# Attention with a mixture of experts: the inverse sums are spread over the partitions by two transfers through DRAM in place of transposes and a copy, with another order of the attention's steps

## The chip, the cores and the metric

The kernel runs on one core of one Trainium2 chip. The metric is the time of one execution on the device, in microseconds. The core has five engines with a queue each: TensorE (PE; its weight loads are PEld), VectorE (DVE), ScalarE (ACT), GpSimd (POOL) and SyncE (SP). They meet in semaphores. 16 DMA engines carry all transfers.

## The reference

One transformer layer on 2048 tokens of 512 values: attention with 16 heads of 128, a layer norm, then a mixture of 64 experts (6 chosen for each token) with shared experts, and a second layer norm. The change touches the attention alone:

```python
k = einsum('ihd,bpd->biph', W_K, x)       # q and v alike
scores = einsum('biph,biqh->biqp', k, q)
masked = scores * tril - 1e10 * (1 - tril)
attn = softmax(masked / sqrt(128), axis=-1)
z = einsum('biqp,biph->biqh', attn, v)
out = einsum('df,bqf->bqd', W_O, z_flat)
```

## The kernel before

The attention runs over eight pairs of heads, `i`, with an unrolled body for each. In a pair, h is the head (0 or 1) and c one of four chunks of 512 queries; (h, c) is a unit, and the units go (0,0), (1,0), (0,1), (1,1), ... (1,3). Every float32 operand is split in a high part and a low part, and each product is three matmuls (high x high, high x low, low x high).

The steps of a pair are:

- "job": projections of q, k and v of a chunk. They write one of four PSUM banks (`bank`), which ScalarE (L375) and VectorE (L466) split.
- "s": a score tile of 128 queries (r) by 512 keys (kc), in a bank too (L606). VectorE takes its maximum (L481), and at the end of a row the maximum of the parts (L487) and its negated, scaled value (L489). "exp" is ScalarE's exponential with the running sum (L391).
- "turn": 128 x 128 transposes of the probabilities of key tile j, up to four, into `turned` (L623). ScalarE copies the high part `pT_hi` (L402), and "lo" is VectorE's low part `pT_lo` (L495). "pv" is the value product of tile j, three matmuls into `z_ps` (L638). A unit of chunk c has 4(c + 1) tiles; the last three of them are cut to 384, 256 and 128 columns by the causal mask.
- "inverse": VectorE adds a unit's sums (L506) and takes the reciprocal (L508), 128 x 4 numbers. They lie with the query on the partition, while `z_ps` has the query along the columns.
- "norm": so TensorE transposes each of the four columns, broadcast to 128 x 128, into a bank (L651), and ScalarE copies the bank to `spread_sb` (L410).
- "out": VectorE multiplies `z_ps` by `spread_sb` into `z_sb` (L516), and SyncE stores it (L336). `z_ps` is one bank: the next unit's first value product waits for this step.

Each engine runs its own share of the steps in the order of one string, `ORDER`: "f" stands for the next projection or score, "e" exp, "t" turn, "l" lo, "p" pv, "i" inverse, "n" norm, "o" out and "w" the split of the next pair's weights. There are no priorities besides it, so what stands behind a waiting instruction on its engine waits too. Chunk 0 of the next pair is projected and scored ahead, in the body before.

SyncE also loads each chunk of x (two transfers of 1 MB, L277 and L278) after the last v projection of the chunk before, and in three of the four places zeroes two or three blocks of `gathered_x`, rows of 527 values, behind them (L322). GpSimd only makes constants in this stage. After the attention comes a stage with the output projection, the routing and the experts, and then the combination of the sums.

Of the kernel before, what the change touches and what calls it, by code (L numbers as in the profile page):

```python
# [7 lines left out]
P = 128  # L8
# [55 lines left out]
def wait_apart(eng, waited, sem, value):  # L64
# [12 lines left out]
    "tttflillffffifnffpteeflfpteffeeeppttolnffleeptffleepfftlepeffpettfeolllffepeitplfiffntlfffffptpetept"  # L77
    "llefflptfppeolfeettffepltfepelftlfpltleeptlenpfpfttlffeepptoetlffpelteefpllftfppelieettptnlflfflptee"
    "ffefflfffffpftppettellptlefppotltlffpleftlptipetpeeelltfpffftleepeletpfffftpleeeeltppfffflttlpeepnel"
    "ottfplletffflpwtpetllpetfleptefplffwwteeepptltfflflpetplfppwieetleettllffppttpltpilnfltlofffpetlppft"  # L80
    "tefellpefffftepelpfttleptllfptptplltptplltptllpnpepo"
# [3 lines left out]
def attention_plan():  # L85
# [7 lines left out]
    for h in range(2):  # L93
# [6 lines left out]
        "n": [("norm", 0, *unit) for unit in units], "o": [("out", 0, *unit) for unit in units],  # L100
# [8 lines left out]
def attention(nc, xT, x_parts, w_qkv, z_dram, gathered_x, sums_dram):  # L109
# [7 lines left out]

    ahead_steps = [step for step in plan if step[1]]
# [6 lines left out]
    jobs = [step for step in plan if step[0] in ("job", "s", "norm")]  # L125
    job_at = counted("job", "s", "norm")
    proj_at, exp_at, lo_at = counted("job"), counted("exp"), counted("lo")
    turn_at, pv_at, unit_at = counted("turn"), counted("pv"), counted("out")
    assert counted("inverse") == unit_at and counted("norm") == unit_at
# [16 lines left out]
    with ExitStack() as ctx:  # L146
# [6 lines left out]
        def sem(name):  # L153
            return ctx.enter_context(nc.semaphore(name))
# [9 lines left out]
        spread_sb = sb("spread_sb", [P, CHUNK], F32)  # L164
# [4 lines left out]
        empty_row = sb("empty_row", [P, ROW], F32)  # L169
# [36 lines left out]
        spread_done = sem("spread_done")  # L206
# [50 lines left out]
        @block.gpsimd  # L257
        def _(pool):
            nc.gpsimd.memset(empty_row[:], 0.0).then_inc(const_step, 1)
            nc.gpsimd.memset(ident[:], 0.0).then_inc(const_step, 1)  # L260
            nc.gpsimd.memset(causal_bf[:], 0.0).then_inc(const_step, 1)
            pool.wait_ge(const_step, 3)

            nc.gpsimd.iota(empty_row[:, TOKEN:TOKEN + 1].bitcast(I32), pattern=[[0, 1]], base=SEQ,
                           channel_multiplier=1).then_inc(pool_const, 1)
# [3 lines left out]
            nc.gpsimd.affine_select(out=causal_bf[:], in_=causal_bf[:], compare_op=ALU.is_ge, fill=MASKED,  # L269
                                    base=0, pattern=[[-1, P]], channel_multiplier=1).then_inc(pool_const, 1)  # L270

        @block.sync
        def _(sp):
# [66 lines left out]
            sp.dma_start(sums_dram[SEQ:SEQ + P], empty_row[:, 0:DM]).then_inc(zero_out, 16)  # L340
            sp.wait_ge(x_in, 32 * (CHUNKS * PAIRS - 1))
            sp.wait_ge(zero_out, 16 * (EXPERTS + 1))
# [4 lines left out]
        def _(act):  # L347
# [23 lines left out]
            act.sem_inc(spread_done, n_units)  # L371
# [33 lines left out]
            def spread(i, h, c):  # L405
                u = unit_at[h, c]
                act.wait_ge(job_ready, upto(i, n_jobs, job_at["norm", h, c]))

                act.wait_ge(z_done, upto(i, n_units, u - 1))
                nc.scalar.activation(spread_sb[:], bank[:, job_at["norm", h, c] % BANKS], ACT.Copy).then_inc(spread_done, 1)  # L410

            def body(i, last):
                for step in steps_of(last):
# [6 lines left out]
                    if step[0] == "norm":  # L420
                        spread(i, *step[2:])
# [15 lines left out]
        def _(dve):  # L437
# [61 lines left out]
            def inverse(i, h, c):  # L499

                u = unit_at[h, c]
                before = (c - 1) % CHUNKS
# [41 lines left out]
        def _(pe):  # L544
# [7 lines left out]
            def take(i, n, last):  # L552
# [9 lines left out]
                elif kind == "norm":  # L562
                    pe.wait_ge(spread_done, upto(i, n_units, unit_at[tuple(old)], m < 0))
# [98 lines left out]
            def body(i, last):  # L662
                for step in steps_of(last):
# [8 lines left out]
                    if step[0] == "norm":  # L672
                        spread(i, *step[2:], last)
# [1294 lines left out]
def post_ln_layer(nc, xT, x_rows, w_qkv, w_o, gate_w, w13, w2, s13, s2, out):  # L1968
# [3 lines left out]
    x_parts = dram("x_parts", [CHUNKS, 2, P, DT * CHUNK])  # L1972
    z_dram = dram("z_dram", [TILES, P, HEADS, P])
# [4 lines left out]
    attention(nc, xT, x_parts, w_qkv, z_dram, gathered_x, sums_dram)  # L1978
# [48 lines left out]
```

## Time and profile before

| | |
|---|---|
| time, median of three runs | 2611.55 us (2609.22 to 2616.04) |
| time of the profiled execution | 2612.08 us |
| its span in the trace | 2610.3 us |
| TensorE busy | 2474.8 us, 95% |
| VectorE busy | 1762.7 us, 68% |
| ScalarE busy | 1454.5 us, 56% |
| GpSimd busy | 268.6 us, 10% |
| mean of the granted TensorE clock | 0.983 |

The busy times are those of the whole span. A time in the trace counts from the start of the span; 1.8 us of the execution lie around it. The attention ends at about 1665 us.

### The profile page before, as it was taken

Reading aid. Unit: us, or ns where it says so; the run is one execution under the profiler, and the core shown is the slowest. Engines: PE = TensorE matmul, PEld = TensorE weight load, DVE = VectorE, ACT = ScalarE, POOL = GpSimd, SP = SyncE. Lnnn points to the kernel's source line nnn. Section 1 sums busy time; section 2 is a strip of 40 time slices with the busy share of each in tenths; the row PEclk is TensorE's granted clock in tenths of the full one; section 3 lists DMA queues with packets and bytes.
Section 4 is the critical chain, followed back from the end, with each engine's and each line's share of the span. In section 5 each row is a group of like instructions: output and inputs, shape, how many; then the busy total and the mean of one; then the engine's idle time right before and its main releaser. Section 6 shows DMA issues by size and latency. Waiting matters only on the chain. (4 is left out here: it accounts for less than half of the span.)

```text
span 2610.3 us, 40937 instructions
## 1 busy us (share of the span) xinstructions
PE 2474.8 (95%) x14304; PEld 2141.0 (82%) x14304; DVE 1762.7 (68%) x3802; ACT 1454.5 (56%) x3247; POOL 268.6 (10%) x221
## 2 busy tenths in 40 slices
PE   6999999999999999999999999798899999999992
PEld 5888888888888888888888888576688889898992
DVE  4666566566566557557567566588867888888884
ACT  3555555455456456456456455444436777777771
POOL 0000000000000000000000000045551112122121
PEclk9999999999999999999999999899999999999996
DMA  6311311310320320311311220367749999999995
GB/s 250 124 49 47 120 49 47 123 51 15 118 88 15 108 86 27 108 54 55 108 58 55 82 66 18 144 219 269 248 134 278 308 295 317 305 299 318 303 310 154
DMA packets 176892, 380.09 MB, mean 146 GB/s; under 512 B 19561, under 2 KB 52457, under 8 KB 166448
## 3 DMA queue, kind: packets, MB, share of 16 engines
q1 hardware_dynamic: 154096, 330.69, 37.4%
q0 software_dynamic: 20288, 42.59, 7.1%
q10 hardware_dynamic: 2304, 4.20, 0.4%
q8 instruction: 115, 1.88, 0.3%
q14 instruction: 89, 0.73, 0.1%
HBM read 279.67 MB, written 106.35 MB: 148 GB/s over the span
## 5 line engine op out<-in xcount | busy, mean ns | idle before, releaser
L402 ACT ACTIVATE pT_hi<-turned 128x512 fp32r<-128x512 f32 (+3 forms) x640 | 330.4, 537 | 292.1 <-PE turned L623 291.1
L495 DVE TENSOR_TENSOR pT_lo<-turned,pT_hi 128x512 fp32r<-128x512 f32 (+3 forms) x640 | 375.5, 604 | 104.9 <-ACT pT_hi L402 102.9
L391 ACT ACTIVATE probs<-bank,neg_max 128x512 f32<-128x512 f32 (+3 forms) x640 | 395.9, 626 | 80.2 <-DVE neg_max L489 76.1
L481 DVE TENSOR_REDUCE max_part<-bank 128x1 f32<-128x512 f32 (+2 forms) x576 | 344.8, 621 | 114.5 <-PE bank L606 103.7
L593 PE MATMUL bank<-x_sb,w_hi 128*128 128x512 f32 x1024 | 323.4, 397 | 20.1 <-ACT ident_bf L366 13.6
L623 PE MATMUL turned<-ident,probs 128*128 128x128 f32 x2176 | 320.5, 273 | 0.3 <-PEq L682 0.3
L623 PEld LDWEIGHTS turned<-ident,probs 128*128 128x128 f32 x2176 | 263.1, 141 | 44.9 <-issue 0.7
L638 PE MATMUL z_ps<-pT_hi,v_hi 128*128 128x512 f32 (+3 forms) x640 | 255.6, 399 | 14.9 <-DVE pT_lo L495 12.4
L606 PE MATMUL bank<-k_lo,q_hi 128*128 128x512 f32 (+2 forms) x640 | 254.2, 397 | 0.0
L606 PE MATMUL bank<-k_hi,q_hi 128*128 128x512 f32 (+2 forms) x640 | 250.3, 391 | 0.0
L1736 DVE TENSOR_TENSOR up_lo<-w_raw,up_hi 128x704 fp32r<-128x704 f32 x256 | 217.3, 887 | 34.3 <-ACT up_hi L1243 33.3
L593 PEld LDWEIGHTS bank<-x_sb,w_hi 128*128 128x128 f32 x1024 | 191.7, 190 | 59.1 <-issue 13.6
L638 PE MATMUL z_ps<-pT_hi,v_lo 128*128 128x512 f32 (+3 forms) x640 | 234.8, 367 | 0.0
L638 PE MATMUL z_ps<-pT_lo,v_hi 128*128 128x512 f32 (+3 forms) x640 | 234.0, 366 | 0.0
L606 PE MATMUL bank<-k_hi,q_lo 128*128 128x512 f32 (+2 forms) x640 | 233.7, 365 | 0.0
L593 PE MATMUL bank<-x_sb,w_lo 128*128 128x512 f32 x512 | 201.4, 393 | 0.0
L582 PE MATMUL bank<-w_hi,x_sb 128*128 128x256 f32 x1024 | 191.8, 284 | 1.7 <-ACT probs L391 1.7
L1243 ACT ACTIVATE up_hi<-w_raw 128x704 fp32r<-128x704 f32 x250 | 185.0, 786 | 3.1 <-DMA w_raw<-in_w 2.7
L977 POOL MEMSET ident<- 128x128 f32 x1 | 0.2, 204 | 1666.3 <-POOLq L146 1666.3
L582 PEld LDWEIGHTS bank<-w_hi,x_sb 128*128 128x128 f32 x1024 | 162.1, 191 | 3.3 <-DVE probs L454 2.1
L638 PEld LDWEIGHTS z_ps<-pT_hi,v_hi 128*128 128x128 f32 x640 | 121.2, 189 | 36.6 <-DVE pT_lo L495 14.1
L1049 POOL DMA_INDIRECT sums_dram<-y_sb,token x64 | 110.0, 1720 | 386.5 <-DMA sums_dram<-y_sb,token 244.1
(211 smaller groups left out, 5259.4 us busy)
## 6 DMA issues: line engine op xcount, KB each, us to landing
w_raw<-in_w SPq DMA_DIRECT2D x256, 352.0 KB, 5.6
x_sb<-x_parts SPq DMA_DIRECT2D x62, 1024.0 KB, 6.0
w_raw<-in_w SPq DMA_DIRECT2D x128, 256.0 KB, 5.7
gathered_x<-empty_row SPq DMA_DIRECT2D x64, 263.5 KB, 9.3
rows_in<-gathered_x SPq DMA_DIRECT2D x64, 263.5 KB, 5.4
z_dram<-z_sb SPq DMA_DIRECT2D x64, 256.0 KB, 2.3
z_raw<-z_dram SPq DMA_DIRECT2D x16, 1024.0 KB, 5.8
w_raw<-in_w_qkv SPq DMA_DIRECT2D x32, 384.0 KB, 10.5
```

Source lines behind the costliest of these rows:

```text
L391: nc.scalar.activation(probs[:, u % 2, r, kc * CHUNK:kc * CHUNK + used], bank[:, job_at["s", h, c, r, kc] % BANKS, 0:used], ACT.Exp, bias= ...
L402: nc.scalar.activation(pT_sb[0][:, n % TURNS, lo_col:], turned[:, n % TURNS, lo_col:], ACT.Copy).then_inc(turn_hi, 1)
L481: nc.vector.reduce_max(max_part[:, row % ROWS, kc:kc + 1], bank[:, job % BANKS, 0:used], axis=AX_X).then_inc(part_done, 1)
L495: nc.vector.tensor_tensor(pT_sb[1][:, n % TURNS, lo_col:], turned[:, n % TURNS, lo_col:], pT_sb[0][:, n % TURNS, lo_col:].bitcast(F32), AL ...
L582: mark = nc.tensor.matmul(dst[:, t * 2 * DH:(t + 1) * 2 * DH], x_sb[:, a, dt, rows_], w_sb[b][:, dt, 4 * DH:], start=(dt == 0 and (a, b) = ...
L593: mark = nc.tensor.matmul(dst, w_sb[a][:, dt, first:first + DH], x_sb[:, b, dt, :], start=(dt == 0 and (a, b) == PASSES[0]), stop=(dt == D ...
L606: mark = nc.tensor.matmul(dst[:, 0:width], q_sb[a][:, h, r * P:(r + 1) * P], k_sb[b][:, h, kc * CHUNK:kc * CHUNK + width], start=(a, b) == ...
L623: mark = nc.tensor.transpose(turned[:, n % TURNS, r * P:(r + 1) * P], probs[:, u % 2, r, j * P:(j + 1) * P], ident[:])
L638: mark = nc.tensor.matmul(z_ps[:, first * P:], v_sb[a][:, j, h * DH:(h + 1) * DH], pT_sb[b][:, n % TURNS, first * P:], start=(j == 0 and ( ...
L1049: nc.gpsimd.indirect_dma_start(sums_dram, bass.IndirectOffsetOnAxis(ap=token4[:, n:n + 1], axis=0), y_sb[:, n % 2], None, bounds_check=las ...
L1243: nc.scalar.activation(dst_of(0, n % 2, p, up_w, down_w), raw_of(raw, q % SLOTS_RAW, p), ACT.Copy).then_inc(w_hi, 1)
L1736: nc.vector.tensor_tensor(dst_of(1, n % 2, p, up_w, down_w), raw_of(raw, q % SLOTS_RAW, p), dst_of(0, n % 2, p, up_w, down_w).bitcast(F32) ...
```

## The change

The step "norm" goes. In its place GpSimd stores the 128 x 4 inverse sums of a unit in a DRAM row of 512 values, waits until they are there, and loads the row into all 128 partitions of `spread_sb`, which now has two buffers. In DRAM the four values of a partition stand side by side, so the z product reads the row with a step of four values for each of its four blocks of 128 columns. The inverse waits for the store of the unit two before in place of the norm's transposes. The zeros that SyncE writes come from a tile of 271 columns in place of 527, so each such transfer becomes two. The order string is another one.

```diff
 ORDER = (
-    "tttflillffffifnffpteeflfpteffeeeppttolnffleeptffleepfftlepeffpettfeolllffepeitplfiffntlfffffptpetept"
+    "tlfiiftfffltlfffpftlfpppoeeefefttetelffpllteffeeplpfeftetepolfltfilfpfeepttelleffffffpffftptilelptfp"
...
-    jobs = [step for step in plan if step[0] in ("job", "s", "norm")]
+    jobs = [step for step in plan if step[0] in ("job", "s")]
...
+            def spread(i, h, c):
+
+                u = unit_at[h, c]
+                per = 16 * n_units // 2
+                wait_apart(pool, waited, inv_done, upto(i, n_units, u))
+                pool.dma_start(inv_dram[u % 2].rearrange("(p r) -> p r", r=RPC), inv[:, u % 2]).then_inc(inv_stored[u % 2], 16)
+                wait_apart(pool, inv_free, inv_stored[u % 2], i * per + 16 * (u // 2 + 1))
+                wait_apart(pool, waited, z_done, upto(i, n_units, u - 2))
+                pool.dma_start(spread_sb[:, u % 2], inv_dram[u % 2:u % 2 + 1].to_broadcast([P, CHUNK])
+                               ).then_inc(spread_in[u % 2], 16)
...
-                            sp.dma_start(gathered_x[bass.ds(e, 1)].rearrange("a p n -> (a p) n"),
-                                         empty_row[:]).then_inc(zero_out, 16)
+                            empty = gathered_x[bass.ds(e, 1)].rearrange("a p n -> (a p) n")
+                            sp.dma_start(empty[:, 0:EMPTY], empty_row[:, 0:EMPTY]).then_inc(zero_out, 16)
+                            sp.dma_start(empty[:, EMPTY:], empty_row[:]).then_inc(zero_out, 16)
...
-            sp.dma_start(sums_dram[SEQ:SEQ + P], empty_row[:, 0:DM]).then_inc(zero_out, 16)
+            for first in range(0, DM, EMPTY):
+                sp.dma_start(sums_dram[SEQ:SEQ + P, first:first + EMPTY], empty_row[:, 0:EMPTY]).then_inc(zero_out, 16)
...
-            def spread(i, h, c):
-                u = unit_at[h, c]
-                act.wait_ge(job_ready, upto(i, n_jobs, job_at["norm", h, c]))
-
-                act.wait_ge(z_done, upto(i, n_units, u - 1))
-                nc.scalar.activation(spread_sb[:], bank[:, job_at["norm", h, c] % BANKS], ACT.Copy).then_inc(spread_done, 1)
...
-                dve.wait_ge(job_ready, upto(i, n_jobs, job_at["norm", h, before], c == 0))
+                dve.wait_ge(inv_free, upto(i, n_units, u - 2))
                 nc.vector.reduce_sum(total[:, u % 2], sums[:, u % 2, :, 0:c + 1], axis=AX_X).then_inc(sum_done, 1)
...
-                dve.wait_ge(spread_done, upto(i, n_units, u))
-
+                dve.wait_ge(spread_in[u % 2], i * (8 * n_units) + 16 * (u // 2 + 1))
                 dve.wait_ge(z_out[u % 2], i * (8 * n_units) + (8 * n_units + 16 * (u // 2)))
-                nc.vector.tensor_tensor(z_sb[:, u % 2], z_ps[:], spread_sb[:], ALU.mult).then_inc(z_done, 1)
+                by_row = spread_sb[:, u % 2].rearrange("p (n r) -> p r n", r=RPC)
+                nc.vector.tensor_tensor(z_sb[:, u % 2].rearrange("p (r n) -> p r n", r=RPC),
+                                        z_ps[:].rearrange("p (r n) -> p r n", r=RPC), by_row, ALU.mult).then_inc(z_done, 1)
...
-            def spread(i, h, c, last):
-
-                u = unit_at[h, c]
-                dst = take(i, job_at["norm", h, c], last)
-                pe.wait_ge(inv_done, upto(i, n_units, u))
-                for r in range(RPC):
-                    mark = nc.tensor.transpose(dst[:, r * P:(r + 1) * P], inv[:, u % 2, r:r + 1].to_broadcast([P, P]),
-                                               ident[:])
-                mark.then_inc(job_ready, 1 + left_out(i, job_at["norm", h, c], last))
```

How the order moves is seen at the end of unit (1, 2), in each pair. TensorE's program has there before, from the last score tile of the first row of unit (1, 3) to the first matmul of the row's successor (the matmuls on `z_ps` of 256 and 128 columns are the value products of the last two tiles of (1, 2)):

```order
L606 MATMUL bank<-k_lo,q_hi 128x256
L606 MATMUL bank<-k_hi,q_lo 128x256
L623 MATMUL turned<-ident,probs 128x128 x5
L638 MATMUL z_ps<-pT_hi,v_hi 128x256
L638 MATMUL z_ps<-pT_lo,v_hi 128x256
L638 MATMUL z_ps<-pT_hi,v_lo 128x256
L638 MATMUL z_ps<-pT_hi,v_hi 128x128
L638 MATMUL z_ps<-pT_lo,v_hi 128x128
L638 MATMUL z_ps<-pT_hi,v_lo 128x128
L651 MATMUL bank<-ident,inv 128x128 x4
L623 MATMUL turned<-ident,probs 128x128 x8
L606 MATMUL bank<-k_hi,q_hi 128x512
```

And after the change, from the same score tile:

```order
L621 MATMUL bank<-k_lo,q_hi 128x256
L621 MATMUL bank<-k_hi,q_lo 128x256
L638 MATMUL turned<-ident,probs 128x128 x4
L653 MATMUL z_ps<-pT_hi,v_hi 128x256
L653 MATMUL z_ps<-pT_lo,v_hi 128x256
L653 MATMUL z_ps<-pT_hi,v_lo 128x256
L638 MATMUL turned<-ident,probs 128x128 x4
L653 MATMUL z_ps<-pT_hi,v_hi 128x128
L653 MATMUL z_ps<-pT_lo,v_hi 128x128
L653 MATMUL z_ps<-pT_hi,v_lo 128x128
L638 MATMUL turned<-ident,probs 128x128 x4
L621 MATMUL bank<-k_hi,q_hi 128x512
```

The four transposes of inv are gone; the transposes of unit (0, 3)'s first tiles are split up among the last two value products.

On VectorE the same place before, from the maxima of that score row to the z product of unit (1, 2); the three `pT_lo` of 256, 128 and 512 columns are tiles 10 and 11 of (1, 2) and tile 0 of (0, 3):

```order
L481 TENSOR_REDUCE max_part<-bank 128x1 [waits job_ready,exp_done]
L481 TENSOR_REDUCE max_part<-bank 128x1 [waits job_ready] x3
L487 TENSOR_REDUCE row_max<-max_part 128x1 [waits part_done]
L489 TENSOR_SCALAR neg_max<-row_max 128x1 [waits max_done]
L495 TENSOR_TENSOR pT_lo<-turned,pT_hi 128x256 [waits turn_hi]
L495 TENSOR_TENSOR pT_lo<-turned,pT_hi 128x128 [waits turn_hi]
L495 TENSOR_TENSOR pT_lo<-turned,pT_hi 128x512 [waits turn_hi]
L516 TENSOR_TENSOR z_sb<-z_ps,spread_sb 128x512 [waits z_out1,spread_done,pv_done]
```

And after:

```order
L498 TENSOR_REDUCE max_part<-bank 128x1 [waits job_ready,exp_done]
L498 TENSOR_REDUCE max_part<-bank 128x1 [waits job_ready]
L512 TENSOR_TENSOR pT_lo<-turned,pT_hi 128x256 [waits turn_hi]
L498 TENSOR_REDUCE max_part<-bank 128x1 [waits job_ready] x2
L504 TENSOR_REDUCE row_max<-max_part 128x1 [waits part_done]
L506 TENSOR_SCALAR neg_max<-row_max 128x1 [waits max_done]
L512 TENSOR_TENSOR pT_lo<-turned,pT_hi 128x128 [waits turn_hi]
L512 TENSOR_TENSOR pT_lo<-turned,pT_hi 128x512 [waits turn_hi]
L532 TENSOR_TENSOR z_sb<-z_ps,spread_sb 128x512 [waits z_out1,spread_in1,pv_done]
```

Tile 10's low part has moved ahead of the last two maxima; the z product waits for `spread_in1`, a transfer, in place of `spread_done`.

## Rows read from the trace of the kernel before

**Rows 1.** Windows: a middle pair, the last pair, and the gap behind it.

```profile
core 0: us, PE busy (x) PEld busy (x) DVE busy (x) ACT busy (x) POOL busy (x), PEclk, DMA share, GB/s
252.80:456.30 203.50, 202.15 (x1203) 172.44 (x1202) 125.25 (x268) 109.92 (x277) 0.00 (x0) 1.00 0.21 71
1473.80:1664.50 190.70, 185.06 (x1075) 156.84 (x1074) 113.51 (x243) 100.18 (x253) 0.00 (x0) 0.98 0.14 45
1664.50:1680.00 15.50, 0.91 (x2) 0.83 (x3) 5.45 (x8) 5.14 (x5) 1.94 (x8) 0.59 0.77 289
```

**Rows 2.** Timeline, PE, the first spread of two pairs (start, us, what).

```profile
270.38 0.28 PE L582 MATMUL bank<-w_hi,x_sb 128*128 128x256 f32 x1
270.49 0.60 PE L651 MATMUL bank<-ident,inv 128*128 128x128 f32 x4
270.85 0.47 PE L606 MATMUL bank<-k_hi,q_hi 128*128 128x512 f32 x1
271.16 0.39 PE L606 MATMUL bank<-k_lo,q_hi 128*128 128x512 f32 x1
271.38 0.39 PE L606 MATMUL bank<-k_hi,q_lo 128*128 128x512 f32 x1
...
473.97 0.60 PE L651 MATMUL bank<-ident,inv 128*128 128x128 f32 x4
```

**Rows 3.** Groups by line, the middle pair from 252.8 us to 456.3 us.

```profile
line engine op names shapes xcount | busy us, mean ns | idle before us <-releasers
...
L638 PEld LDWEIGHTS z_ps<-pT_hi,v_hi 128*128 128x128 f32 x80 | 15.1, 189 | 3.9 <-DVE pT_lo L495 1.6 <-issue 0.8 <-DVE z_sb L516 0.3
...
L516 DVE TENSOR_TENSOR z_sb<-z_ps,spread_sb 128x512 f32<-128x512 f32 x8 | 5.5, 686 | 2.4 <-issue 1.3 <-PE z_ps L638 1.0
...
L410 ACT ACTIVATE spread_sb<-bank 128x512 f32<-128x512 f32 x9 | 5.4, 605 | 1.6 <-PE bank L651 1.4
```

**Rows 4.** Timeline, end of unit (1, 2) in that pair; in brackets the idle time.

```profile
390.27 0.71 PE L623 MATMUL turned<-ident,probs 128*128 128x128 f32 x5
...
391.11 0.15 DVE L489 TENSOR_SCALAR neg_max<-row_max 128x1 f32<-128x1 f32 x1
391.18 1.21 DVE L495 TENSOR_TENSOR pT_lo<-turned,pT_hi 128x256 fp32r<-128x256 f32 x3
...
391.65 0.39 PE L638 MATMUL z_ps<-pT_hi,v_hi 128*128 128x256 f32 x1 [0.67 <-DVE pT_lo L495]
...
392.39 0.62 PE L651 MATMUL bank<-ident,inv 128*128 128x128 f32 x4
...
392.85 1.04 PE L623 MATMUL turned<-ident,probs 128*128 128x128 f32 x8
...
393.05 0.60 ACT L410 ACTIVATE spread_sb<-bank 128x512 f32<-128x512 f32 x1
...
393.73 0.69 DVE L516 TENSOR_TENSOR z_sb<-z_ps,spread_sb 128x512 f32<-128x512 f32 x1 [1.34 <-issue]
...
394.48 0.19 PEld L638 LDWEIGHTS z_ps<-pT_hi,v_hi 128*128 128x128 f32 x1 [0.33 <-DVE z_sb L516]
```

**Rows 5.** Line 996: GpSimd's plain loads (192 to 352 KB), later stage.

```profile
L996 POOL DMA_DIRECT2D s_raw<-in_s x14: 559/593/782, 1669.9 to 1878.8; - x14
...
DMA to landing us min/median/max: 3.1/4.1/6.6
```

**Rows 6.** Lines 336 (store of z) and 322 (zeros), issue and landing.

```profile
L336 SPq DMA_DIRECT2D z_dram<-z_sb x64: 359/371/378, 74.7 to 1665.2; - x64
...
DMA to landing us min/median/max: 2.3/2.3/8.9
...
DMA to landing us min/median/max: 2.3/9.3/10.7
```

**Rows 7.** Timeline, end of the attention.

```profile
1663.14 0.29 DVE L495 TENSOR_TENSOR pT_lo<-turned,pT_hi 128x128 fp32r<-128x128 f32 x1 [0.28 <-ACT pT_hi L402]
...
1664.12 0.27 PE L638 MATMUL z_ps<-pT_hi,v_lo 128*128 128x128 f32 x1
1664.48 0.69 DVE L516 TENSOR_TENSOR z_sb<-z_ps,spread_sb 128x512 f32<-128x512 f32 x1 [1.04 <-PE z_ps L638]
...
1665.60 0.51 SPq L340 DMA_DIRECT2D sums_dram<-empty_row  x1
```

More of the change, by code:

```diff
@@ L76 @@
 ORDER = (
-    "tttflillffffifnffpteeflfpteffeeeppttolnffleeptffleepfftlepeffpettfeolllffepeitplfiffntlfffffptpetept"
[L78 to L81, printed above, removed]
+    "tlfiiftfffltlfffpftlfpppoeeefefttetelffpllteffeeplpfeftetepolfltfilfpfeepttelleffffffpffftptilelptfp"
+    "lfeetfelppoefettffelepetfplffltpeetlfpffeltpeftplleftfeeppottlfllefpetpfleeepfttpffeitleellfffffffff"
+    "fptptlpetpeetlepltffplfftlelpeetpetofflpfltflptpeetlpieflpfetfltfpteepltptllffppeetlfftpleltpoeltfep"
+    "tlfeplffwtpetpllwtlefptpeltfelpftfiwpeetelptflfeptlflfwepeppteetlltlffpptptlotfplltfffppetlfetfelile"
+    "pffffetlfppttlleepftptllptptplltlptpltelpppo"
 )
@@ L99, in attention_plan @@
         "p": [("pv", 0, *tile) for tile in tiles], "i": [("inverse", 0, *unit) for unit in units],
-        "n": [("norm", 0, *unit) for unit in units], "o": [("out", 0, *unit) for unit in units],
+        "o": [("out", 0, *unit) for unit in units],
         "w": [("wsplit", 0, dt) for dt in range(DT)],
@@ L106, in attention_plan, with attention @@
     return plan, units
-def attention(nc, xT, x_parts, w_qkv, z_dram, gathered_x, sums_dram):
+def attention(nc, xT, x_parts, w_qkv, inv_dram, z_dram, gathered_x, sums_dram):
     plan, units = attention_plan()
@@ L116, in attention @@
     ROWS = 4
+    EMPTY = DM // 2
     ahead_steps = [step for step in plan if step[1]]
@@ L122, in counted @@
                 for n, step in enumerate(step for step in plan if step[0] in kinds)}
-    jobs = [step for step in plan if step[0] in ("job", "s", "norm")]
-    job_at = counted("job", "s", "norm")
+    jobs = [step for step in plan if step[0] in ("job", "s")]
+    job_at = counted("job", "s")
     proj_at, exp_at, lo_at = counted("job"), counted("exp"), counted("lo")
     turn_at, pv_at, unit_at = counted("turn"), counted("pv"), counted("out")
-    assert counted("inverse") == unit_at and counted("norm") == unit_at
+    assert counted("inverse") == unit_at
     rows = [step[2:5] for step in plan if step[0] == "s" and step[5] == 0]
@@ L163, in attention @@
         pT_sb = [sb(f"pT_{n}", [P, TURNS, CHUNK], F32R) for n in ("hi", "lo")]
-        spread_sb = sb("spread_sb", [P, CHUNK], F32)
+        spread_sb = sb("spread_sb", [P, 2, CHUNK], F32)
         z_sb = sb("z_sb", [P, 2, CHUNK], F32)
@@ L168, in attention @@
         causal_bf = sb("causal_bf", [P, P], BF16)
-        empty_row = sb("empty_row", [P, ROW], F32)
+        empty_row = sb("empty_row", [P, ROW - EMPTY], F32)
         max_part = sb("max_part", [P, ROWS, CHUNKS], F32)
@@ L205, in attention @@
         inv_done = sem("inv_done")
-        spread_done = sem("spread_done")
+        inv_stored = [sem(f"inv_stored{n}") for n in range(2)]
+        inv_free = sem("inv_free")
+        spread_in = [sem(f"spread_in{n}") for n in range(2)]
+        waited = sem("waited1")
         z_done = sem("z_done")
@@ L270, in _, with body @@
                                     base=0, pattern=[[-1, P]], channel_multiplier=1).then_inc(pool_const, 1)
+            pool.sem_inc(inv_free, n_units)
+            def spread(i, h, c):
[7 more added lines that the diff above has]
+                               ).then_inc(spread_in[u % 2], 16)
+            def body(i):
+                for step in plan:
+                    if step[0] == "inverse":
+                        spread(i, *step[2:])
+            for i in range(PAIRS):
+                body(i)
         @block.sync
@@ L370, in _ @@
             act.sem_inc(turn_hi, n_turns)
-            act.sem_inc(spread_done, n_units)
             def project(i, job):
@@ L419, in body @@
                         turn(i, *step[2:])
-                    if step[0] == "norm":
-                        spread(i, *step[2:])
                     if step[0] == "wsplit" and not last:
@@ L561, in take @@
                     pe.wait_ge(exp_done, upto(i, n_exp, exp_at[tuple(old)], m < 0))
-                elif kind == "norm":
-                    pe.wait_ge(spread_done, upto(i, n_units, unit_at[tuple(old)], m < 0))
                 else:
@@ L671, in body @@
                         value(i, *step[2:])
-                    if step[0] == "norm":
-                        spread(i, *step[2:], last)
             for step in ahead_steps:
@@ L1972, in post_ln_layer @@
     x_parts = dram("x_parts", [CHUNKS, 2, P, DT * CHUNK])
+    inv_dram = dram("inv_dram", [2, CHUNK])
     z_dram = dram("z_dram", [TILES, P, HEADS, P])
@@ L1977, in post_ln_layer @@
     x1T_parts = dram("x1T_parts", [TILES, 2, P, DT * P])
-    attention(nc, xT, x_parts, w_qkv, z_dram, gathered_x, sums_dram)
+    attention(nc, xT, x_parts, w_qkv, inv_dram, z_dram, gathered_x, sums_dram)
     route_and_experts(nc, z_dram, w_o, gate_w, x_rows, w13, w2, s13, s2, sums_dram, x1T_parts, gathered_x)
```

5 lines of the change are left out of this document (2 added, 3 removed).

## Prediction

> **What bounds the kernel now.** I read the windows first. One of the middle pairs of heads takes 203.5 us, and TensorE is busy for 202.15 us of them, VectorE for 125.25 and ScalarE for 109.92, at a granted clock of 1.00, which is the 2.4 GHz level [rows 1]. The period of a pair is seen a second time in the starts of the same block of transposes, 270.49 and 473.97: 203.48 us [rows 2]. So between 60 and 1640 us the end is set by what TensorE has in its queue. Work that leaves its queue is won in full; work that leaves VectorE or ScalarE is won only where TensorE waits for them.
>
> Then the timeline, because busy time of matmuls is modelled and hides short waits. The distance from one start to the next tells more. In a pair these distances leave about 2.4 us that are no work, and all of it stands at one place, the end of unit (h 1, chunk 2). The piece of it shown in [rows 4] reads so: five transposes are issued at 390.27, and the next in the queue, the value matmul of tile 10 (256 columns), starts at 391.65, with 0.67 us shown as idle. The five need 0.11 us each (four take 0.45 in the row at 392.39), so 0.83 us are lost. The reason stands between: VectorE finishes the maximum of a score row first (the negated maximum, 391.11) and only then makes tile 10's low part (391.18), because its program has the row's four maxima ahead of it. A second, smaller wait comes behind it: the z product starts at 393.73, when the copy of the spread has ended (393.05 plus 0.60), and TensorE's next value matmul starts at 394.48, which is 0.3 us late. The grouped row of one pair says the same: 1.6 us of waiting for pT_lo, 0.8 put down to issue, 0.3 for z_sb [rows 3].
>
> **What goes, and what it costs today.** The spread is four transposes in each of 64 units. [Rows 2]: they start at 270.49, the next matmul at 270.85, so 0.36 us; and that matmul is followed by the next at 271.16, 0.31 us later, where the one after it has 0.22 or 0.23: another 0.08. Together 0.44 us. In the other setting, between transposes, it is 392.39 to 392.85, 0.46 us [rows 4]. I take 0.44: 64 x 0.44 = **28.2 us** off TensorE's queue, all of it on the path, since the queue is 99% full. Eight bank slots in a pair go too, which can only relax the ring of four banks.
>
> ScalarE loses 64 copies of 0.605 us [rows 3], 39 us, or 4.8 us of a pair's 110. It is 46% idle there, so this is worth nothing by itself; it shortens the answers for which TensorE waits at the place above.
>
> **What comes.** Two transfers per unit, issued by GpSimd, which has no other work in this stage (busy 0.00 in [rows 1]). Nothing that TensorE does waits for them directly: the z product on VectorE does, and behind it VectorE's whole queue, and the next unit's first value matmul. So the question is whether they land in the time between the inverse and the z product. In the new list the shortest such stretch is unit (1, chunk 2): six score tiles of 0.69 us (three passes of 0.23), one of 0.82 and one of 0.48, five value tiles of 0.69 and three cut ones of 0.53, 0.36 and 0.32, and transposes for 2.86 us at 0.11 each: 13.0 us of TensorE's work. The next is unit (0, chunk 3), 16.5 us; the others have 18.8 to 29.7. In the last pair, where the steps ahead are missing, units of chunk 3 have 11.1 and 11.9 us plus the waits of that tail.
>
> The trace has no transfer of either kind, so I bound the chain. Below: the fastest store of z, 2.3 us [rows 6], and the fastest GpSimd load, 3.1 us [rows 5]: 5.4. Above: 8.9 and 6.6 us, with two issues of 0.78: 17.1. The slow end of the store belongs to one that is queued behind the loads of x and three zero transfers, which themselves take 9.3 us in the median and at most 10.7 to land [rows 6]; in the new list the inverse of (1, chunk 2) stands 19 us behind the last such burst. So I take a quiet store of 3, a median load of 4.1 and two issues of 0.59: about **8.3 us**, hidden in 13.0 and in 11.1. Cost 0. If the cover were gone, each microsecond over 13.0 would cost 8 us.
>
> VectorE's z product changes shape: it reads the spread with a step of four floats. Today it takes 0.686 us [rows 3]. No row has such a read. Below, it costs nothing (a read with a step has no less to do, so no gain); above, it costs as much again as the product's own streaming: the pT_lo product of 128 columns takes 0.28 to 0.29 and z's of 512 takes 0.69 [rows 7], so 384 columns are 0.40 and 512 are 0.53 us. It matters only where the product is waited for. At the end of the attention the last matmul starts at 1664.12 and the product at 1664.48 [rows 7], 0.36 later; with its 0.69 and 0.06 for the hand-over the next unit's first value matmul can start 1.1 us after the last one's start. The new list puts 0.11 + 1.13 = 1.24 us of work there after unit (1, chunk 2), and 1.8 or more after the others: just enough at 0.69, 0.4 us short at 1.22. I take 0 to 0.4 per pair, 0.2 in the middle: 1.6 us.
>
> Against this stands a rule of the Trainium skill ("SBUF — State Buffer", section "Door 1: The DMA port swizzle", the note on cachelines): SBUF has lines of 16 bytes, full speed needs at least two hits in a line, and each access to a new line pays. A step of four floats meets a new line with every element. By it the product would be at the upper end and the sum 1.6 us higher (an estimate); no row here shows it.
>
> **What moves.** The list is another one, so the 2.4 us of waiting in a pair are drawn anew. On VectorE two of the four maxima of row (1, chunk 3, r 0) now stand behind the low part of tile 10 instead of ahead of it, which takes away the 0.9 us of [rows 4]. The low part of tile 11 still stands behind the row's negated maximum, while TensorE has its value matmul 1.2 us behind that score: I count 0.3 to 0.4 us there. On TensorE the transposes of a tile and the value matmul that needs them stand under 2 us apart in 6 places of a pair instead of 10. That speaks for about 1 us a pair rather than 2.4. But a new list can have places of its own that I don't see from positions, so I count only half of the difference and of that what the z product leaves: 2.4 - 1.6 = 0.8 us a pair, eight times, **6 us**. The product's 0.2 is in these 1.6.
>
> SyncE issues 64 more zero transfers (about 0.5 us each) behind the loads of x. The stores of z behind them come up to 1.6 us later, with two buffers of z and at least 9 us to the next store that needs one: 0. At the very end one more such transfer is issued after the last store: the one that is there starts at 1665.60, takes 0.51 us [rows 7], and the stage's end waits for it: +0.4 us.
>
> **Sum.** The profiled execution took 2612.1 us (0.5 over the median of the three runs shown, 2611.55). 2612.1 - 28.2 - 6 + 0.4 = 2578.3; against the median, 2577.8. I say **2578**.
>
> **Rivals.**
> *The waits all go.* With 0.2 us left in a pair the list is worth 17.6 instead of 6: 2566.5. For it: all waits of today stand at one place, and the list loosens it. Against: tile 11 there. 20 in 100.
> *The saved work is won, but the z product is slow or the list waits as before.* 2612.1 - 28.2 + 0.4 + 8 x 0.4 = 2587.5. For it: the step of four floats and the 1.24 us. 18 in 100.
> *The list has new waits of 3 us a pair on top of today's,* for example where the turn of unit (0, chunk 3) stands 1.3 us behind the exp of its last row instead of 4.1. Then -28.2 + 24: 2608, within 0.3% of no change. 5 in 100.
> *The transfers come too late,* the rival on the other side. VectorE stands at the z product of (1, chunk 2) and (0, chunk 3) while TensorE runs dry behind it. With a chain of L the cost of a pair is (L - 13.0) + (L - 16.5) over zero. It eats the 28.2 us at L = 16.5 and makes the kernel slower by over 0.3% from L = 17.0; at 18 it costs 52 us, and the time is 2636. For it: 128 descriptors that all read the same 2 KB of DRAM, which no row has, and 128 pieces of 16 bytes in the store. Against: L must be twice my value, and the upper bound from rows is 17.1. 7 in 100.
> That the change doesn't do what it says has nothing for it: no transposes of inv are left on TensorE.
>
> **How the numbers follow.** The forecast has 50 in 100. A difference under 0.3%, 8 us, could not be told from none. The range of the forecast alone is 2572 to 2584; to leave out no more than 2 in 10 it takes in the two rivals beside it: 2565 to 2592. Faster 0.88, same 0.05, slower 0.07.
>
> **What the profile of the changed kernel would show.** A pair's window of about 199.5 us with TensorE busy for all but 1 to 2 of them. z product at 0.69 us or up to 1.2. GpSimd's spread landing in 3 to 5 us, its store in 2 to 4, and no idle time of VectorE ahead of the z product that ends with a landing; if there is such a row with more than 0.5 us each, the rival on the other side is at work. The prediction is wrong if the pair's period falls by less than 3.5 us: then a wait took the place of the transposes, and the idle column of the value matmuls names it.

## The result and the profile after

The changed kernel takes 2575.84 us (median of 4; 2568.45 to 2578.61) against 2613.8 us (4 runs) of the kernel before: a ratio of 0.986, 95% interval 0.9841 to 0.9879. Forecast were 2578 and a range of 2565 to 2592. The profiled execution took 2573.6 us with a span of 2571.8.

The windows of a middle pair and of the last pair, with the columns of [rows 1]:

```profile
core 0: us, PE busy (x) PEld busy (x) DVE busy (x) ACT busy (x) POOL busy (x), PEclk, DMA share, GB/s
248.18:446.64 198.46, 198.40 (x1170) 169.40 (x1170) 127.52 (x268) 106.08 (x269) 8.63 (x16) 1.00 0.27 83
1439.00:1621.50 182.50, 179.73 (x1043) 152.07 (x1041) 116.48 (x243) 95.50 (x242) 8.63 (x16) 0.99 0.20 59
```

A pair is 5.0 us shorter (203.5 in [rows 1]) and TensorE shows hardly any idle time in it. VectorE has 2.3 us more work, ScalarE 3.8 less, GpSimd 16 issues. The same pair by line, which answers to [rows 3]:

```profile
line engine op names shapes xcount | busy us, mean ns | idle before us <-releasers
...
L653 PEld LDWEIGHTS z_ps<-pT_hi,v_hi 128*128 128x128 f32 x80 | 15.1, 189 | 2.3 <-DVE z_sb L532 0.5 <-DVE pT_lo L512 0.4
...
L532 DVE TENSOR_TENSOR z_sb<-z_ps,spread_sb 128x512 f32<-128x512 f32 x8 | 8.6, 1081 | 0.9 <-PE z_ps L653 0.8
```

The z product takes 1.08 us in place of 0.69, and its engine never waits for a transfer ahead of it. Of the 3.9 us of idle time ahead of the weight loads of the value matmuls in [rows 3], 2.3 are left; of the part put down to VectorE, 0.9 in place of 1.9. The end of unit (1, 2), as in [rows 4] (timeline):

```profile
383.12 0.36 PE L653 MATMUL z_ps<-pT_hi,v_hi 128*128 128x256 f32 x1
...
383.67 1.05 DVE L512 TENSOR_TENSOR pT_lo<-turned,pT_hi 128x128 fp32r<-128x128 f32 x2
...
384.01 0.33 PE L653 MATMUL z_ps<-pT_hi,v_hi 128*128 128x128 f32 x1
...
384.64 1.08 DVE L532 TENSOR_TENSOR z_sb<-z_ps,spread_sb 128x512 f32<-128x512 f32 x1
...
385.32 0.40 PE L621 MATMUL bank<-k_hi,q_lo 128*128 128x512 f32 x1
...
385.77 0.50 PE L653 MATMUL z_ps<-pT_hi,v_hi 128*128 128x512 f32 x1
```

Tile 10's value matmul (383.12) comes without the 0.83 us wait. The one wait left at this place is at 385.77: 0.45 us after the matmul before it, where 0.23 would do, because the z product ends at 385.72.

The transfers of that unit (timeline):

```profile
371.18 0.18 DVE L524 RECIPROCAL inv<-total 128x4 f32<-128x4 f32 x1
371.93 0.54 POOL L283 DMA_DIRECT2D inv_dram<-inv  x1 [31.71 <-DVE inv L524]
374.29 0.54 POOL L286 DMA_DIRECT2D spread_sb<-inv_dram  x1 [1.82 <-DMA inv_dram<-inv]
```

Over all 64 units, from issue to landing, the store first, then the load:

```profile
DMA to landing us min/median/max: 1.7/1.7/8.4
...
DMA to landing us min/median/max: 3.3/3.5/4.4
```

The reciprocal ends at 371.36 and the spread lands at 374.29 + 3.5 = 377.8: a chain of 6.4 us, while the z product starts 13.3 us behind the reciprocal (its cover). That is a quiet unit. Unit (1, 1) of the same pair stores its sums right behind two loads of x and six transfers of zeros, issued from 301.9 to 305.4 us; the DMA share is 0.92 from 306 to 314 us (timeline):

```profile
305.35 0.18 DVE L524 RECIPROCAL inv<-total 128x4 f32<-128x4 f32 x1
306.11 0.54 POOL L283 DMA_DIRECT2D inv_dram<-inv  x1 [18.58 <-DVE inv L524]
314.26 0.54 POOL L286 DMA_DIRECT2D spread_sb<-inv_dram  x1 [7.62 <-DMA inv_dram<-inv]
325.68 1.09 DVE L532 TENSOR_TENSOR z_sb<-z_ps,spread_sb 128x512 f32<-128x512 f32 x1
```

Its store takes 7.5 us to land, the chain is 12.2 us long and the cover 20.2. The longest chain of the pairs looked at is that of (1, 0) in the last pair, 14.9 us under a cover of 26.0: it stands behind the chain of (0, 0) in GpSimd's queue.

The attention ends (end of the last z product) at 1622.0 us in place of 1665.2, 43 us earlier, but the execution is 38.5 us shorter. Some 3 of the 43 us are the granted clock of the one execution that was traced before. Its last pair holds two stretches at 0.50; the kernel with the split zeros alone (an experiment below), whose attention is otherwise the one of before, has none in its last pair and ends it at 1662.6 us:

```profile
1640.10:1643.50 3.40, 3.40 (x18) 3.30 (x16) 1.24 (x4) 1.10 (x3) 0.00 (x0) 0.50 0.00 0
1646.90:1650.30 3.40, 3.40 (x11) 2.70 (x11) 0.66 (x1) 0.60 (x1) 0.00 (x0) 0.50 0.27 77
...
1471.20:1661.90 190.70, 185.11 (x1096) 156.97 (x1094) 115.30 (x246) 101.68 (x256) 0.00 (x0) 1.00 0.16 51
```

From 1662.6 it is 40.6 us. What lies behind the attention took 945.2 us in the trace of before and 949.9 in this one; the last experiment comes back to this.

### The profile page after: what moved, and what is told of

The parts are those of the page before. It is cut to its first block and busy times, and to the rows that moved or that the text cites. A ratio compares the mean times of both kernels' runs of the same rounds, so it can differ in the third digit from the quotient of the medians.

```text
span 2571.8 us, 40617 instructions
## 1 busy us (share of the span) xinstructions
PE 2444.0 (95%) x14048; PEld 2115.2 (82%) x14048; DVE 1778.3 (69%) x3802; ACT 1423.4 (55%) x3183; POOL 339.3 (13%) x349
## 5 line engine op out<-in xcount | busy, mean ns | idle before, releaser
L608 PE MATMUL bank<-x_sb,w_hi 128*128 128x512 f32 x1024 | 323.9, 398 | 20.0 <-ACT ident_bf L393 13.3
L638 PE MATMUL turned<-ident,probs 128*128 128x128 f32 x2176 | 329.2, 273 | 0.1
L283 POOL DMA_DIRECT2D inv_dram<-inv x64 | 34.9, 546 | 1350.7 <-DVE inv L524 1350.7
L597 PE MATMUL bank<-w_lo,x_sb 128*128 128x256 f32 x512 | 145.5, 284 | 0.0
```

The costliest lines, as they stand in the source:

```text
L597: mark = nc.tensor.matmul(dst[:, t * 2 * DH:(t + 1) * 2 * DH], x_sb[:, a, dt, rows_], w_sb[b][:, dt, 4 * DH:], start=(dt == 0 and (a, b) = ...
L608: mark = nc.tensor.matmul(dst, w_sb[a][:, dt, first:first + DH], x_sb[:, b, dt, :], start=(dt == 0 and (a, b) == PASSES[0]), stop=(dt == D ...
L638: mark = nc.tensor.transpose(turned[:, n % TURNS, r * P:(r + 1) * P], probs[:, u % 2, r, j * P:(j + 1) * P], ident[:])
```

## The experiments

The times of a kernel spread by 10 us, the period of a pair in one trace hardly at all as long as no transfer is late: it was 203.48 us before and 198.46 now, again and again. So the period is compared, measured from a projection of v to the same one of the next pair, and the times stand beside it.

**The transfers alone.** The changed kernel with the order string of before, its eight "n" taken out:

```diff
-    "tlfiiftfffltlfffpftlfpppoeeefefttetelffpllteffeeplpfeftetepolfltfilfpfeepttelleffffffpffftptilelptfp"
+    "tttflillffffifffpteeflfpteffeeeppttolffleeptffleepfftlepeffpettfeolllffepeitplfifftlfffffptpeteptlle"
```

> The changed kernel with the order of before (its eight n taken out), so the transfers without the new list. If TensorE's queue is what counts and the list is a term of its own: the period of a middle pair is 203.5 - 3.5 = 200.0 us, perhaps 0.3 more for the slower z product, and the time about 2612 - 28 = 2584, some 9 to 12 us over the changed kernel. If the whole gain came from the list and the transposes had been hidden: 2612 and a period of 203.5. If the transfers only do no harm thanks to the new list (late ones in the old): over 2600, with idle time of VectorE at the z product that ends with a landing.

Measured: 2589.9 us, ratio 0.9913 (0.9894 to 0.9932). The window of a pair:

```profile
260.76:461.12 200.36, 198.96 (x1169) 169.15 (x1168) 127.32 (x268) 105.85 (x268) 8.65 (x16) 1.00 0.28 83
```

3.12 us less than before. The 0.83 us wait of [rows 4] is there again, and so are the other waits for pT_lo (1.6 us in the pair ahead of the weight loads, as in [rows 3]). The end of unit (1, 2) (timeline):

```profile
384.60 0.71 PE L638 MATMUL turned<-ident,probs 128*128 128x128 f32 x5
385.97 0.39 PE L653 MATMUL z_ps<-pT_hi,v_hi 128*128 128x256 f32 x1 [0.67 <-DVE pT_lo L512]
...
386.60 0.28 PE L653 MATMUL z_ps<-pT_hi,v_lo 128*128 128x128 f32 x1
...
386.91 1.11 DVE L532 TENSOR_TENSOR z_sb<-z_ps,spread_sb 128x512 f32<-128x512 f32 x1 [0.20 <-PE z_ps L653]
...
388.07 0.40 PE L621 MATMUL bank<-k_hi,q_lo 128*128 128x512 f32 x1
388.30 0.40 PE L653 MATMUL z_ps<-pT_hi,v_hi 128*128 128x512 f32 x1
```

But the wait for the z product is gone here: it starts 0.31 us after the unit's last value matmul, where it stood behind ScalarE's copy before (393.73 in [rows 4]), and the next value matmul follows in 0.23 us although the product is slower. That gives 0.2 us back. A new wait of 0.3 us stands at 274.92, at the first value matmul of unit (1, 0): TensorE comes there earlier, without the transposes, and VectorE's low part ends 0.4 us later, behind the slower product of (0, 0). The list is a term of its own, of 200.36 - 198.46 = 1.90 us a pair.

**The transposes doubled,** in the kernel before:

```diff
-                for r in range(RPC):
+                for r in (*range(RPC), *range(RPC)):
```

> The kernel before with the four transposes of the spread issued twice. If each block of four costs its whole 0.44 us of TensorE's queue: period 203.5 + 3.5 = 207.0 us and time 2612 + 28 = 2640. If part of the block lies in waits that are there anyway (TensorE waits 2.4 us in a pair): less, down to 2612 + 20. If the transposes were hidden: 2612.

Measured: 2638.2 us, ratio 1.0087 (1.0068 to 1.0105).

```profile
269.27:476.24 206.97, 205.63 (x1234) 175.91 (x1232) 125.20 (x268) 109.95 (x276) 0.00 (x0) 1.00 0.21 70
```

3.49 us more, 0.436 per block of four: the sum's 0.44. Adding (3.49) and taking away (3.12, and 0.1 for the waits that changed) agree within 0.3 us.

**The list alone.** The kernel before with the new order. It needs eight "n" in it, and they take a place in the ring of four banks. I placed them twice:

```diff
-    "tttflillffffifnffpteeflfpteffeeeppttolnffleeptffleepfftlepeffpettfeolllffepeitplfiffntlfffffptpetept"
+    "tlfiiftnfffltlfffpftlfpppoeneefefttetelffpllteffeeplpfeftetepolfltfilfpfeeptntelleffffffpffftptilelp"
```

> The kernel before (transposes and copy) with the new order, n put in where the bank ring allows it. The list as a term of its own: the period falls by the waiting that it removes, 203.5 - 1.5 = 202.0 us, and the time to about 2600. If the list pays only together with the transfers (because ScalarE has less to do, and no bank is taken): 2609 to 2616, period 203 or more, and the 0.9 us waits of tile 10 come back or move.

Measured: 2668.3 us, ratio 1.0207 (1.0188 to 1.0226), period 211.3. Neither expectation held: TensorE waited for exponentials that free a bank, right at the "n". One such place (timeline):

```profile
425.05 0.40 PE L606 MATMUL bank<-k_hi,q_lo 128*128 128x512 f32 x1
427.80 1.11 PE L651 MATMUL bank<-ident,inv 128*128 128x128 f32 x4 [2.35 <-ACT probs L391]
428.55 0.78 PE L638 MATMUL z_ps<-pT_hi,v_hi 128*128 128x512 f32 x1
429.13 0.63 PE L638 MATMUL z_ps<-pT_lo,v_hi 128*128 128x512 f32 x1
```

> Again the kernel before (transposes and copy) with the new order, but each n later, where the ring of four banks is least strained. In the run before TensorE waited for exponentials that free a bank at six places, 8 us a pair, right where the n stood. If that was the place of the n alone: period 202 to 202.5 us, 2600 to 2605. If the new list needs the ring without the eight spread jobs: the waits for exponentials come back elsewhere and the period stays over 204.

Measured with the later places: 2609.0 us, ratio 1.0008 (0.9994 to 1.0022), period 203.8, no better than before. The expectation's second branch, with a period over 204, fits in kind, but not quite in size. The waits for pT_lo are gone (0.2 us in place of 1.6), but others stand around the spread of (1, 2):

```profile
393.63 0.65 PE L651 MATMUL bank<-ident,inv 128*128 128x128 f32 x4 [0.56 <-ACT probs L391]
...
395.64 0.50 PE L606 MATMUL bank<-k_hi,q_hi 128*128 128x512 f32 x1 [0.61 <-ACT probs L391]
```

So with these places of "n" the new list is worth nothing while the spread takes a bank, and 1.9 us a pair once it takes none. Whether some other placement would have kept a part of it is open; 2 of many were tried. Nor is it shown whether the bank or ScalarE's eight copies (0.6 us each) make the exponentials late here: both runs have both.

**The step of four.** The store writes column by column, so that the z product reads its row packed:

```diff
-                pool.dma_start(inv_dram[u % 2].rearrange("(p r) -> p r", r=RPC), inv[:, u % 2]).then_inc(inv_stored[u % 2], 16)
+                pool.dma_start(inv_dram[u % 2].rearrange("(r p) -> p r", r=RPC), inv[:, u % 2], allow_slow_non_contiguous=True).then_inc(inv_stored[u % 2], 16)
...
+                nc.vector.tensor_tensor(z_sb[:, u % 2], z_ps[:], spread_sb[:, u % 2], ALU.mult).then_inc(z_done, 1)
```

> The changed kernel, but the store writes the 128 x 4 numbers column by column (512 pieces of 4 bytes), so that the z product reads its row packed. If the step of four floats makes the product slow: 0.69 us in place of 1.08, the 0.2 us wait of TensorE for the z product goes, period 198.46 - 0.2 to 0.3 us, time 2 us lower, within the measurement. If the product is slow for another reason: it stays at 1.08 and nothing moves. If the store of 4-byte pieces takes over 6 us longer than the 1.7 of now, the chain outlasts the cover and the period grows.

Measured: 2630.6 us, ratio 1.0095 (1.0073 to 1.0117), period 206.4 in the middle pair. The product takes 0.69 us again. The edit takes away the step of four and, with it, the pattern of four blocks in which the product named its operands, so the 0.39 us belong to the two together; no run has one without the other. And the store now lands after 8.5 us in the median:

```profile
256.96 0.76 POOL L283 DMA_DIRECT2D inv_dram<-inv  x1 [15.25 <-DVE inv L524]
266.31 0.55 POOL L286 DMA_DIRECT2D spread_sb<-inv_dram  x1 [8.58 <-DMA inv_dram<-inv]
266.85 0.76 POOL L283 DMA_DIRECT2D inv_dram<-inv  x1
273.58 0.69 DVE L531 TENSOR_TENSOR z_sb<-z_ps,spread_sb 128x512 f32<-128x512 f32 x1
278.87 0.54 POOL L286 DMA_DIRECT2D spread_sb<-inv_dram  x1 [11.26 <-issue]
287.25 0.69 DVE L531 TENSOR_TENSOR z_sb<-z_ps,spread_sb 128x512 f32<-128x512 f32 x1 [4.74 <-DMA spread_sb<-inv_dram]
```

The worst unit is not the one with the shortest cover. (0, 0) and (1, 0) have their inverses at the same place in the list, and GpSimd, which waits for each store before it issues the load, works them off one after the other: the second store is issued 9.9 us after the first, and the z product of (1, 0) waits 4.74 us. That is not the pair's whole loss of 8.0 us. TensorE also waited 1.7 us for a late load of x, and from 287.2 to 294.0 us its granted clock was 0.50; over the pair it is idle for 5.1 us and its matmuls are busy 2.9 us longer than the changed kernel's:

```profile
263.12:469.54 206.42, 201.32 (x1169) 171.26 (x1168) 124.85 (x268) 106.01 (x268) 10.41 (x16) 0.98 0.31 80
```

Other pairs of this trace take 200.7 to 209.4 us.

**The chain made longer.** The changed kernel with the load done two and four times, each waiting for the one before (here with one more load; the other has three more):

```diff
+                for more in range(1):
+                    pool.dma_start(spread_sb[:, u % 2], inv_dram[u % 2:u % 2 + 1].to_broadcast([P, CHUNK])
+                                   ).then_inc(hop, 16)
+                    wait_apart(pool, waited, hop, 16 * ((i * n_units + u) * 1 + more + 1))
```

> The changed kernel with each spread load done twice, one after the other, so that the chain from inverse to landed spread grows from 6.4 to about 10.5 us. If there are 13.0 us of cover as counted: no change, 2576 and a period of 198.5. If the cover is thinner than counted (other work of VectorE late, or transfers in each other's way): over 2580.

Measured: 2580.3 us, ratio 0.9899 (0.988 to 0.9919). Period 198.46 in the pair shown first, as in the changed kernel, but not in all:

```profile
260.35:458.81 198.46, 198.41 (x1170) 169.41 (x1169) 127.50 (x268) 106.22 (x268) 12.92 (x24) 1.00 0.30 94
855.64:1057.36 201.72, 198.62 (x1170) 169.32 (x1168) 127.56 (x268) 106.14 (x268) 12.93 (x24) 1.00 0.30 93
```

In the second VectorE waits 3.9 us for a spread. The loads that end a chain land after 3.4 us in the median, 8.3 at most. The cover holds a chain of 10.5 us in most pairs, with little to spare: 3.0 us in unit (1, 2), and in (1, 0), whose two chains in a row take 24.7 of its 26.0 us, 1.3.

> The same with four loads, a chain of about 18.7 us. By the sum of the prediction's slower rival: (18.7 - 13.0) + (18.7 - 16.5) = 7.9 us a pair, so a period of 206.4 and a time of about 2576 + 63 = 2639; VectorE idle ahead of the z product until a landing in two of eight units. If VectorE's wait is partly made up by other work: less, 2600 to 2630. If the wait idles TensorE long enough to lower its granted clock: more, over 2650.

Measured: 2872.2 us, ratio 1.1022 (1.0999 to 1.1046), over four times the expected loss. The window of a pair:

```profile
295.33:527.81 232.48, 206.55 (x1169) 174.48 (x1168) 127.23 (x268) 106.01 (x268) 21.50 (x40) 0.94 0.32 98
```

And the z products of this pair, by line:

```profile
L537 DVE TENSOR_TENSOR z_sb<-z_ps,spread_sb 128x512 f32<-128x512 f32 x8 | 8.5, 1059 | 34.1 <-DMA spread_sb<-inv_dram 34.1
```

VectorE waits 34.1 us for the spread, and the pair has lost 34.0 us: the mechanism is the rival's. But the two are not the same microseconds. On TensorE the loss is 25.9 us of idle time and 8.1 us of longer matmuls, at a mean granted clock of 0.94 over the pair; the rival's sum had no such term, while the expectation's last sentence did. And its count of waits was too small: at chunk 0 two chains queue up on GpSimd, and the first meets the loads of x (timeline, the end of the first chain and of the second):

```profile
308.67 0.54 POOL L291 DMA_DIRECT2D spread_sb<-inv_dram  x1 [6.82 <-DMA spread_sb<-inv_dram]
309.20 0.54 POOL L284 DMA_DIRECT2D inv_dram<-inv  x1
316.67 1.05 DVE L537 TENSOR_TENSOR z_sb<-z_ps,spread_sb 128x512 f32<-128x512 f32 x1 [10.95 <-DMA spread_sb<-inv_dram]
...
333.07 1.05 DVE L537 TENSOR_TENSOR z_sb<-z_ps,spread_sb 128x512 f32<-128x512 f32 x1 [5.42 <-DMA spread_sb<-inv_dram]
```

Of the 34 us, 16.4 are these two units. The rest, 17.7, is four other units, (1, 1), (1, 2), (0, 3) and (1, 3), whose chains of 18 to 25 us outlast covers of 13 to 20.

**Chain against cover, and a better version.** The packed product with six inverses moved forward in the list, and the same with the old store and product for the two units of chunk 0:

```diff
-    "tlfiiftfffltlfffpftlfpppoeeefefttetelffpllteffeeplpfeftetepolfltfilfpfeepttelleffffffpffftptilelptfp"
+    "tlfiiftfffltlfffpftlfpppoeeefefttetelffpllteffeeplpfefteitepolfltflfpfeepttelleffffffpffftptleliptfp"
...
+                form = "(p r) -> p r" if c == 0 else "(r p) -> p r"
```

> The packed product of e5, with six of the eight inverses of a pair moved forward in the list (the two of chunk 0 can't go further), so that the counted cover is 19.8 to 41 us in place of 13.0 to 29.7. If e5 was slow because its chain of some 14.5 us outlasted the cover: the wait of unit (1, 2) goes and what stays is unit (1, 0), whose chain queues behind that of (0, 0) on GpSimd (29 us for 27.9): a period of 199 to 203 us, 2580 to 2610. If the 512 small pieces slow other work: VectorE's waits for the spread go but the period stays over 204.

Measured: 2606.2 us, ratio 0.9972 (0.9959 to 0.9986), period 201.7. The wait of unit (1, 2) is gone; VectorE waits 4.0 us in the pair for a spread, all of it at (1, 0), and that makes up the 3.3 us that this version is behind the next one. The pair is one of the middling ones: periods run from 200.1 to 206.7 us, and in the pair from 659.8 us (205.6) it is unit (0, 0) that waits, 4.28 us.

> As e9, but the two units of chunk 0 keep the store and the product with the step of four, whose chain is 6.4 us. By the reading of chain against cover no unit waits for a transfer, and TensorE's 0.2 us wait for the z product is gone: period 198.1 to 198.3 us, the best so far by 0.2 to 0.4 us a pair, 2 to 3 us in all, less than the times can tell. If the late landings of e5 had another cause, they are here again: over 200.

Measured: 2574.5 us, ratio 0.9864 (0.9842 to 0.9886), and in the pair from 459 us

```profile
459.24:657.59 198.35, 198.35 (x1170) 169.32 (x1168) 125.34 (x268) 105.99 (x268) 9.99 (x16) 1.00 0.29 83
```

No product waits for a transfer. This pair is 0.1 us better than the changed kernel's, less than the 0.2 to 0.4 expected, and it is not every pair: the two before it, from z product to z product, take 199.07 and 199.05 us, with a wait of TensorE for an exponential in them that the pair shown does not have:

```profile
320.40 0.50 PE L625 MATMUL bank<-k_hi,q_hi 128*128 128x512 f32 x1 [0.43 <-ACT probs L418]
```

Over the seven periods the mean is 198.5 us in both kernels. The moved list wins nothing.

**The split zeros alone,** in the kernel before:

```diff
-                            sp.dma_start(gathered_x[bass.ds(e, 1)].rearrange("a p n -> (a p) n"),
-                                         empty_row[:]).then_inc(zero_out, 16)
+                            sp.dma_start(empty[:, 0:EMPTY], empty_row[:, 0:EMPTY]).then_inc(zero_out, 16)
+                            sp.dma_start(empty[:, EMPTY:], empty_row[:]).then_inc(zero_out, 16)
```

> The kernel before with the zero transfers split in two and nothing else. Prediction's term: 0.4 us at the end, nothing elsewhere, so a period of 203.5 and 2612. If the split transfers (1 KB rows in place of 2.1 KB) lengthen the bursts so that loads of x come late: a wait of TensorE for x_sb and a longer period.

Measured: 2612.0 us, ratio 1.0012 (0.9997 to 1.0027), period 203.47. Nothing.

**The changed kernel again.**

> The changed kernel once more, unchanged, beside the others. Period 198.46 us, the attention's end at 1622 us. The part behind the attention took 950 us in its trace and 945 in that of before, and 943 to 954 in the experiments: if that is chance, another value in this range; if the change costs something there, 948 or more again.

Measured: 2577.1 us, ratio 0.9862 (0.9838 to 0.9886), period 198.43, end of the attention at 1621.3 us. Behind it 958.9 us, 9 more than in the first trace of the same kernel: one trace tells little of that part, which took between 942.0 us (split zeros) and 958.9 over all of them. But the expectation named "948 or more again" as the sign of a cost, and 958.9 is that. The medians say more. Take from a kernel's median time the 1.8 us around the span and the end of the attention in its trace, and what is left is 944.1 (before), 942.9, 943.6, 944.2 and 947.6 us in the five kernels without the two transfers, and 948.2, 950.7, 951.1, 952.0, 952.3, 953.6, 954.0 and 957.6 in those with them (the changed kernel: 952.0 and 954.0). The groups do not overlap. That speaks for a cost of some 3 to 8 us (an estimate from these medians) behind the attention that goes with the change, although the code there is the same but for the zeros written to `sums_dram` at the attention's end. It is not shown: the working takes for granted that the attention ends in the untraced executions when it does in the traced one, and the medians of the kernel before differ by 5.7 us between the rounds of runs (2608.24 to 2613.96). No run shows a cause. In the traces most of the difference arises in the loop over the experts.

## Why the prediction was right

*The transposes.* 28.2 us forecast. Taken away they gave 3.12 us a pair together with the slower product (25 us in all), doubled they cost 3.49 a pair, eight times 27.9 us. Reading a block's cost from starts (0.36 until the next matmul, 0.08 in the one behind) rather than from its busy time (32 x 0.273 overlapping matmuls, 4.8 us a pair) is what made this right.

*ScalarE's copies at nothing.* Nearly held. On the old list the waits for pT_lo stayed as they were without the copies; but the z product of (1, 2) no longer stood behind one, and the 0.2 us that TensorE waited for it went.

*The transfers, hidden.* Chain 8.3 us forecast, 6.4 measured in the quiet units; cover in (1, 2) 13.0 counted from the list, 13.3 measured, in (0, 3) 16.5 and 15.8. The store was overrated (1.7 us, not 3), the load too (3.5, not 4.1). One value was not right for all units: (1, 1) has 12.2 us and (1, 0) up to 14.9. They stayed hidden because these two have 20 and 26 us of cover; at the cover of (1, 2) a chain of 14.9 would have shown.

*The z product.* 0.69 to 1.22 us as bounds, 1.08 measured; the wait that it causes was put at 0.2 us a pair in the middle and is 0.2 in the changed kernel, 0.3 at another place on the old list. The Trainium skill's rule on 16-byte lines ("SBUF — State Buffer", "Door 1: The DMA port swizzle") agrees in direction: with the step 0.39 us more for 512 elements, and the packed read takes them back. That the line is the reason, and not the pattern of four blocks, is not shown.

*The list.* This term was mis-sized. Forecast: 6 us for the list less the product's waits. Measured: 198.46 against 203.48 - 3.49 = 199.99, so 1.5 us a pair, 12 us. (The 0.8 us a pair behind the 6 did not follow from its own working either: half of the difference between 1.0 and 2.4 is 0.7, and less the product's 0.2 it is 0.5, or 4 us. The rival in which all waits go adds up to 2566.7, not 2566.5.) The low part of tile 11, for which I had counted 0.3 to 0.4 us, cost at most 0.1, and no new waits of any size came. What I had not seen: that gain depends on the other half of the change. The new order with the spread still in the bank ring gave nothing in one placement and lost 54 us in the other.

*The rival on the other side* had the right mechanism and the wrong price. It summed cover by unit as though each had its own queue. Two chains that start together share GpSimd, so (1, 0) with 26 us of cover is as tight as (1, 2) with 13; a chain of about 14 us already costs 8 us a pair (packed product, 206.42 against 198.46), where the rival's sum gives 1. It also had no term for the granted clock, which fell to 0.50 after such a wait (2.9 us of these 8), nor for the load of x that came late (1.7 us of waiting).

*The sum.* The prediction took 33.8 us off. The attention gave 5.02 us x 8 = 40 us; the 3 more in the trace are the clock in the last pair of the execution before. The time shows 38.0, and 33.9 in the second measurement (2577.12 against 2611.06). So the mechanism was right, and that 2578 lies 2 us from the median is partly luck: the list gave 6 us more than its term, and 2 to 6 us are missing again behind the attention, where the prediction had nothing.

## What to carry to other kernels

Where one engine's queue is full, an operation's worth is its start-to-start time in that queue, and taking it out and doubling it should give the same number. A transfer chain is free as long as it is shorter than its cover, but chains that wait inside one issuing queue add up, so count the cover for all that start together, and take the chain's length from each unit and not from the median one. An order found for a kernel belongs to its resources: judge it with the operations and the rings that it will run with. A stage's end in one trace can be off by a few microseconds of granted clock: read the periods, and compare what is left of the time with all runs.

## What was not expected of the hardware

- 512 pieces of 4 bytes to DRAM land 8.5 us after the issue, 128 pieces of 16 bytes (the same 2 KB) after 1.7 us; 128 reads of one 2 KB row into 128 partitions take 3.5 us. All three are medians; behind other transfers the store of 16-byte pieces took up to 8.4 us.
- After a wait of 2.75 us between matmul starts (425.05 to 427.80 above) TensorE's next matmuls of 512 columns stood 0.43 us apart, not 0.23, until 431.2; the granted clock from 427.8 to 431.2 is 0.51, which is the lower of its two levels. So a long wait can cost more than itself: with four loads, PEclk is 0.94 over a pair and TensorE is busy 206.6 us with the same matmuls in place of 198.4. The two low stretches at the end of the attention in the trace of before (1640.1 and 1646.9) also stand behind waits: TensorE was busy for 1.97 us of the 4.1 ahead of the first and for 1.34 of the 3.4 ahead of the second. It does not fall every time: the trace with the split zeros alone has 5.6 us of idle time in its last pair as well (190.70 less 185.11), and no low stretch.
